# Row scores in two pairs of PSUM banks, column scores in two banks

## The reference

```python
q = einsum('oc,bct->bot', Wq, layernorm(x)) + bq      # b = 8, o = 256, t = 512
k = einsum('oc,bcs->bos', Wk, ctx) + bk
v = einsum('oc,bcs->bos', Wv, ctx) + bv
# 16 heads of 16 rows each
dot = einsum('bhdt,bhds->bhts', q, k) / 4             # (8, 16, 512, 512)
dot = mask * dot - (1 - mask) * 1e6
amap = softmax(dot, axis=-1) * mask
x = x + einsum('bhts,bhds->bhdt', amap, v)
```

## Time and profile before

| | |
|---|---|
| median of 3 runs | 1535.26 us (1531.8 to 1535.34) |
| profiled execution | 1524.93 us, its span 1523.1 us |
| PE busy | 1390.8 us (91%) |
| DVE busy | 1031.6 us (68%) |
| ACT busy | 592.7 us (39%) |
| POOL busy | 276.1 us (18%) |
| granted TensorE clock, mean | 0.979 |

### The profile page before, as it was taken

The page is one execution under the profiler, slowest core; times in us unless marked ns, Lnnn a source line. Parts: engine busy times, 40 slices in busy tenths (PEclk is TensorE's granted clock), DMA queues, the critical chain, the costliest instruction groups (busy, mean ns, idle before and its releaser), DMA issues.

```text
span 1523.1 us, 23289 instructions
## 1 busy us (share of the span) xinstructions
PE 1390.8 (91%) x8981; PEld 811.0 (53%) x9010; DVE 1031.6 (68%) x1826; ACT 592.7 (39%) x925; POOL 276.1 (18%) x495
## 2 busy tenths in 40 slices
PE   3799899899999999988898799899998999989998
PEld 1344333333333333322676577677776777767776
DVE  9987778878787887875795945654446535465353
ACT  4567366655665565555262111122111221112310
POOL 5014062533536263310000000000000000000000
PEclk9999899999999999999999999999999999999999
DMA  5012223333434333320743401000010000110000
GB/s 176 6 32 78 81 64 108 111 115 95 133 98 148 115 113 98 101 81 15 252 130 114 133 29 56 1 29 1 15 66 5 28 1 1 46 39 29 1 2 28
DMA packets 66466, 105.64 MB, mean 69 GB/s; under 512 B 13359, under 2 KB 38071, under 8 KB 66343
## 3 DMA queue, kind: packets, MB, share of 16 engines
q1 hardware_dynamic: 65335, 103.77, 21.6%
q0 software_dynamic: 1024, 0.40, 0.1%
HBM read 82.40 MB, written 21.35 MB: 68 GB/s over the span
## 4 chain that ended last, share of the span: by engine, by line
PE 34%; DVE 12%; DMA 4%; ACT 1%; issue 1%; POOL 0%; SPq 0%; DVEq 0%; POOLq 0%; ACTq 0%
PE double L1584 10%; PE double L1598 10%; PE double L1610 5%; PE double L1620 2%; PE double L1663 2%; PE double L1631 2%; DMA x_early<-scr_x 2%; DVE f1w L1920 1%; DMA out_x<-x_early 1%; PE double L1650 1%; DVE hid L1824 1%; DVE hv L1822 1%; DVE gate L1821 1%; PE double L1568 1%; ACT th L1708 1%
## 5 line engine op out<-in xcount | busy, mean ns | idle before, releaser
L1162 DVE TENSOR_REDUCE nmx<-level 128x1 f32<-128x512 f32 x512 | 320.1, 681 | 52.9 <-PE level L828 52.0
L920 ACT ACTIVATE prob<-level 128x512 f32<-128x512 f32 x512 | 267.7, 593 | 136.6 <-PE level L837 136.2
L828 PE MATMUL level<-Ks,Qs 105*128 105x512 bf16 x512 | 201.0, 395 | 21.3 <-DVE nmx L1162 20.1
L1708 ACT ACTIVATE th<-double 128x512 f32<-128x512 f32 x96 | 53.9, 562 | 414.1 <-PE double L1584 204.8
L837 PE MATMUL level<-Qs,Ks 108*128 108x512 bf16 x512 | 194.9, 384 | 1.0 <-ACT prob L920 0.8
L1584 PE MATMUL double<-x_parts,f0w 128*128 128x256 f16 x1408 | 157.1, 274 | 5.4 <-DVE hid L1824 2.5
L1584 PE MATMUL double<-x_parts,f1w 128*128 128x256 f16 x1408 | 155.0, 273 | 2.7 <-DVE x_parts L1809 2.7
L1584 PEld LDWEIGHTS double<-x_parts,f0w 128*128 128x128 bf16 x1408 | 137.8, 98 | 24.9 <-issue 3.9
L365 PE MATMUL level<-prob,x_parts 128*128 128x448 bf16 (+1 forms) x527 | 118.3, 378 | 33.4 <-ACT prob L317 15.2
L1584 PEld LDWEIGHTS double<-x_parts,f1w 128*128 128x128 bf16 x1408 | 137.6, 98 | 20.7 <-DVE x_parts L1809 3.1
L1770 POOL TENSOR_TENSOR rstd<-meanvar,halfpow 128x2 f32<-128x2 f32 x22 | 15.2, 691 | 725.9 <-DVE meanvar L1790 725.9
(11 more groups left out here) (206 smaller groups left out, 1893.9 us busy)
## 6 DMA issues: line engine op xcount, KB each, us to landing
scr_q<-qp SPq DMA_DIRECT2D x16, 384.0 KB, 9.3
scr_k<-qp SPq DMA_DIRECT2D x16, 384.0 KB, 3.1
Qs<-scr_q SPq DMA_DIRECT2D x32, 192.0 KB
Ks<-scr_k SPq DMA_DIRECT2D x32, 192.0 KB
hid<-in_f1w1t SPq DMA_DIRECT2D x8, 704.0 KB, 5.8
hid<-in_f1w2t SPq DMA_DIRECT2D x8, 704.0 KB, 4.2
xin<-in_x SPq DMA_DIRECT2D x8, 512.0 KB, 13.2
cx<-in_ctx SPq DMA_DIRECT2D x8, 512.0 KB, 13.7
```

The source lines that it names most:

```text
L828: nc.tensor.matmul(pA[n % 3], Qs[0:MAX_ROW, g, j, P * tt:P * (tt + 1)], Ks[0:MAX_ROW, g, j, :], start=True, stop=True).then_inc(s["a_pe"], 1)
L920: nc.scalar.activation(prob[:, c, j, :], pB[(64 * b + 16 * g + 4 * c + j) % 3], ACT.Exp).then_inc(s["exp_done"], 1)
L1162: nc.vector.tensor_reduce(nmx[:, g % 2, u // 4, u % 4:u % 4 + 1], pA[(64 * b + 16 * g + u) % 3], AX.X, ALU.max, negate=True).then_inc(s["m ...
L1708: y = nc.scalar.activation(th[:, 0:m, :], src[:, 0:m, 0:S], ACT.Tanh, scale=0.5 / XS)
```

## The change

Of the six banks the rows now take four, as two pairs, and the columns two. A maxima instruction reads two banks (128 x 2 x 512) and writes two columns of nmx, so there are 256 in place of 512, and max_done counts pairs. TensorE waits for maxima before even row scores only, for the pair before last. A column score waits for exponential n-2.

```diff
-        level = [W["level"][i][:, c, :] for i in range(2) for c in range(3)]
-        pA, pB = level[0:3], level[3:6]
+        pA = [W["level"][i][:, 0:2, :] for i in range(2)]
+        pB = [W["level"][i][:, 2, :] for i in range(2)]
...
-                    pe.wait_ge(s["max_done"], 64 * B)
+                    pe.wait_ge(s["max_done"], 32 * B)
...
-                wait(pe, s["max_done"], n - 2)
+                if u % 2 == 0:
+                    wait(pe, s["max_done"], n // 2 - 1)
                 j, tt = u // 4, u % 4
-                nc.tensor.matmul(pA[n % 3], Qs[0:MAX_ROW, g, j, P * tt:P * (tt + 1)], Ks[0:MAX_ROW, g, j, :],
+                nc.tensor.matmul(pA[n // 2 % 2][:, n % 2, :], Qs[0:MAX_ROW, g, j, P * tt:P * (tt + 1)], Ks[0:MAX_ROW, g, j, :],
...
-                wait(pe, s["exp_done"], n - 2)
-                nc.tensor.matmul(pB[n % 3], Ks[:, g, j, P * c:P * (c + 1)], Qs[:, g, j, :],
+                wait(pe, s["exp_done"], n - 1)
+                nc.tensor.matmul(pB[n % 2], Ks[:, g, j, P * c:P * (c + 1)], Qs[:, g, j, :],
...
-                    nc.scalar.activation(prob[:, c, j, :], pB[(64 * b + 16 * g + 4 * c + j) % 3], ACT.Exp).then_inc(s["exp_done"], 1)
+                    nc.scalar.activation(prob[:, c, j, :], pB[(64 * b + 16 * g + 4 * c + j) % 2], ACT.Exp).then_inc(s["exp_done"], 1)
...
-                for u in range(u0, u0 + n):
-                    dve.wait_ge(s["a_pe"], 64 * b + 16 * g + u + 1)
+                for u in range(u0, u0 + n, 2):
+                    dve.wait_ge(s["a_pe"], 64 * b + 16 * g + u + 2)
                     if u == 0:
                         wait(dve, s["nmp_done"], 4 * b + g - 1)
-                    nc.vector.tensor_reduce(nmx[:, g % 2, u // 4, u % 4:u % 4 + 1], pA[(64 * b + 16 * g + u) % 3], AX.X, ALU.max,
-                                            negate=True).then_inc(s["max_done"], 1)
+                    nc.vector.tensor_reduce(nmx[:, g % 2, u // 4, u % 4:u % 4 + 2], pA[(32 * b + 8 * g + u // 2) % 2], AX.X,
+                                            ALU.max, negate=True).then_inc(s["max_done"], 1)
...
-                dve.wait_ge(s["max_done"], 16 * (e + 1))
+                dve.wait_ge(s["max_done"], 8 * (e + 1))
```

## The result

The changed kernel takes 1537.1 us in the median of 20 runs, the kernel before beside it 1531.8 us in 20: a ratio of 1.0038, 95% interval 1.0025 to 1.0051. It is slower by 0.38%, as forecast (0.37%), and 1537 lies in the range. The kernel before took 1531.8 us here and not the 1535.3 to which the sum was added, so the forecast is better judged by the difference (5.7 us) than by its 1541. One execution of the last experiment, of 4932 us, stands apart from all others, has no cause in what I measured, and is left out of its comparison.

The account below looks back on a forecast made before the run. TensorE was taken to set the pace unless something holds a matmul. Sequence 0 0.9, sequences 1 to 5 1.5, sequence 6 0.8 and sequence 7 2.5 make 5.7 us; added to 1535.3 they give 1541 us, range 1532 to 1546.

Parts of the forecast that it names:

- The pair's price: On VectorE, a paired reduction runs 1.21 us and occupies 1.13 in place of 1.20; bounds 1.06 and 1.36.
- The odd rows go free: Four odd row matmuls behind VectorE's normalisation, 1.01, 0.88, 0.25 and 1.06 us late before, no longer wait.
- The column waits: First columns of 12 step starts wait for exponentials: 0.38 behind nrow, 0.40 behind U, 0.25 plain; 3.8 us a sequence.
- The replay: Both chains stepped together from 417.29, step (1,1), to the sequence's end: its last column comes 0.30 us late.
- The anchor: Second output transpose at (0,3), tied through xres load to previous sequence's end; rival that it lets go: 1537 us, chance 0.25.
- the drift of 0.3 us a sequence: Sign to look for: the last column of each sequence drifting some 0.3 us a sequence.
- The first sequence: Sequence 0, without anchor or normalisation at (0,2): 0.30 + 0.38 + 0.25 = 0.9 us more.
- The last sequence: Sequence 7, one held row and no rows from (2,1), where both columns of step starts wait: 2.5 us more.
- a longer pair: Rival: on VectorE a pair takes 1.36 us, no shorter than two reductions; 1545 us, chance 0.12.
- The late end of the pair: Rival: maxima reach the nm jobs 0.37 us later; all 32 paying gives 11.8 us, 1553 us, chance 0.05.
- faster: Rival: row waits go while column waits fall where TensorE would stand anyway; 1520 us, chance 0.08.
- sum of 4.7 us to gain and 3.8 to lose: Per sequence: 4.7 us of row-side lateness as possible gain, 3.8 us of new column waits as cost.

Follow-up runs that it names:

- the last experiment: Single maxima in four row banks, row-row-column-column first halves, earlier xres load, statistics behind the first half of (1,0), against the kernel before: ratio 0.9866.
- e3: Changed kernel with the first half of each step ordered row, column, row, column: ratio 0.9979 to the kernel before.
- e4: Changed kernel with each step's first half row, row, column, column and second column, column, row, row: ratio 0.9964 to the kernel before.
- e5: Kernel before with the load of xres issued ahead of the last group's fill: ratio 0.9914 to the kernel before.
- e6: Changed kernel with the load of xres issued ahead of the last group's fill: ratio 0.9962 to the kernel before.
- e2: Changed kernel's banks without pairs: rows in a ring of four with 512 single maxima, columns in two; ratio 1.0007 to the kernel before.
- e1: Kernel before with columns in two banks, rows left at three with single maxima, one bank unused: ratio 1.0043 to the kernel before.
- e11: Kernel before (three and three banks, old order) with earlier xres load and statistics moved behind (2,3): ratio 0.9919 to the kernel before.

## Why the prediction was right, and where its sum was not

- **The pair's price:** 1.21 us taken, 1.22 measured, 1.13 apart as taken. The bound of 1.36 is out.
- **The odd rows go free:** right, all four. The row waits left are those of one even row, 0.58 late by the replay and 0.64 in the trace.
- **The column waits:** three kinds, 0.38, 0.40 and 0.25 us; measured in sequence 3 as 0.34, 0.39 and 0.19 to 0.28, at the nine steps named in the stretch and the three outside it. e3 and e4 show that their cause is the 0.88 us between the columns.
- **The replay:** shifted by 2.87 us it gave 422.42, 425.99, 432.89 and 434.17 for three values groups and nm; the trace has 422.39, 425.98, 432.98 and 434.21. Its 0.30 us to the last column came out as 0.38, in each of sequences 0 to 5. 0.8 us for sequence 6 is 0.79.
- **The anchor:** the mechanism is shown by e5 and e6, and VectorE still waits for the load seven times (12.5 us in all, 14.2 before). But it is the term that was mis-sized. I took the way behind the last column as fixed. It varies from sequence to sequence (19.1 to 20.8 us before, 19.0 to 20.0 after), and on this execution it came out shorter, by 2.5 us over six sequences, so that sequences 1 to 6 together added 0.2 us and not 2.3: the drift of 0.3 us a sequence that I had named as a sign didn't show. Whether that is chance or the change, one execution of each doesn't settle. From one sequence with 0.3 us of waiting I had also concluded that TensorE hardly stands behind this residual; in sequence 7 it stood 4.9 us.
- **The first sequence:** 1.7 us and not 0.9. Its (1,0) has no output transposes before it, so one more plain wait (0.28 us) stands there, and the q job at (0,0) was 0.4 us longer, with TensorE at a lower granted clock (0.57 against 0.78 from 194 to 198 us). The two column waits at (0,2) and (0,3) were in the sum. I had missed the first; nothing ties the second to the change.
- **The last sequence:** 2.5 us predicted. Counted from the first row score, the last column of sequence 7 stands 4.45 us later than before and that of sequence 6 1.93: 2.5 found. It is made of 2.9 from (1,0) on and 0.4 less on the way there, which the sum had not apart.
- **Sum:** 0.1 + 1.7 + 0.2 + 2.5 = 4.5 us in the stage (0.1 is the prologue), where 5.7 stood. One term was 0.8 us too small and one 2.1 too large; that the sum is as near as it is is partly luck. That the ratio of the runs gives 5.8 us (3.8 to 7.8) agrees with both, and so it doesn't tell them apart.
- **The rivals:** a longer pair is out. The late end of the pair is real (e2), 0.29 us a stretch and not 0.37 at each of 32 places. The anchor held, and e6 shows that a period without it costs nothing: 0.15 us less, where that rival had 0.37 less. For faster, the column waits would have had to be half of what they were.

What the sum of 4.7 us to gain and 3.8 to lose hides is how far the two are the same waits. The columns' two banks alone cost 0.64 us a stretch (e1), since most column waits take the place of row waits; the fourth row bank gives 0.55 back (e2), and the pairs cost 0.29 (the changed kernel). The replay had these together and was right; the gain that I put down to the freed odd rows alone was partly the columns' doing.

## What to carry to other kernels

When banks go from one consumer to another, write down for both the distance in time between a producer and the one that needs its bank, with what stands between; here 0.88 us against 1.07 decided, and turning two instructions round was worth more than any split of the six banks. Don't add up waits of two chains that one engine serves in turn: replay them. And before a saving is counted, look for the transfer whose issue hangs on the end of the last round; and when a piece of work is moved on a loaded engine, move it to where that engine stands idle, not to where its neighbour is busy.

## What the runs showed of the hardware

- The third stage, which the change doesn't touch, took 801.3 us in the profiled execution before and 804.6 after. The records of the granted clock hold 26.9 us at 1.2 GHz (half of the full 2.4) in it before and 36.9 after; e1, with 30.9, took 0.7 us more than before, and e3, with 36.3, took 2.8. e11, which has the banks of the kernel before, took 805.7. In 30 runs of the kernel before on one chip, times go from 1518.8 us at a mean clock of 0.980 to 1533.8 at 0.968. The means over runs are the same with the change's edits (0.973 in the changed kernel, 0.974 in e1 and e2) as without (0.973). So this looks like scatter, larger than the change, and not like a part of it.
- A reduction over two PSUM banks, 128 x 2 x 512, took 1.22 us, one over 1024 elements in SBUF 1.21: crossing from one bank into the next shows no cost. A pair in place of two single maxima saves VectorE 2 x 0.60 - 1.13 = 0.07 us. The Trainium skill (Perfetto Trace Analysis, Optimizing Scalar/DVE Operations) gives about 125 ns of access overhead for a VectorE instruction on PSUM; here one instruction fewer saves about half of that.
- Small VectorE operations on 16 elements a partition have two lengths: `nmp` (L1178) took 0.17 us at 433.89 and 1.02 at 418.58, longer than the maximum over a bank. In the changed kernel 14 of its 32 are long. At each of them GpSimd had begun a tensor_tensor of 512 elements (L997) 0.18 us earlier, and VectorE's operation ended 0.03 to 0.04 us after it; none of the 18 short ones began while such an operation ran. Its mean is 0.54 us here, and 0.18 before and in e1 and e2, where GpSimd's operation began just behind it. But other small operations (the two casts beside it, the product for `rs`) are on average longer before than here, and these five groups together take 46 us before and 49 after: the change mostly moved which of them meets GpSimd. No matmul of sequence 3 waits for a long `nmp`, since nm goes without delay at (0,1) and (1,1). That the one engine holds the other up is what the times suggest; no run tested it.
